# Rotary attention in a small transformer tower: which engine copies the transposed probabilities out of PSUM

## The chip, the cores and the metric

One core of a Trainium2 chip runs the whole program in one launch. The metric is the device time of one execution in microseconds; a kernel's time is the median of its runs.

## The reference

The input is 128 images. Each is cut into L = 82 overlapping patches and becomes 82 rows of D = 64 numbers. Four blocks follow, each added to its input and fed with a LayerNorm of it: an attention with relu in place of softmax, a mixture of 6 experts, an attention with rotary positions, and a mixture of 8 experts. The change touches the rotary attention alone. For one image, cut to what matters:

```python
q = concat([c_q @ Wqc, rope(c_q @ Wqr)])        # 48 plain and 16 rotated columns
k = concat([c_kv @ Wkc, rope(c_kv @ Wkr)])
v = c_kv @ Wv
wei = where(causal, q @ k.T / sqrt(64), -inf)   # 82 x 82
out = softmax(wei) @ v
```

All of it is in fp32.

## The kernel before, in words

The rows of all images stay in SBUF, in `h` (82 partitions, 128 images, 64 columns). Each stage walks through NG = 16 groups of G = 8 images. The program is written out by hand for every engine: each stage has one generator per engine (`scalar`, `tensor`, `vector`, `gpsimd`), which issues instructions in a fixed order and waits on semaphores. `build` steps these generators with `go`, so that the end of one stage is interleaved with the start of the next on each engine. An engine works strictly in its own order; a wait at its head holds up all that is behind it.

The rotary attention is `stage_rope_attention`. In iteration g the engines do the following, each in this order.

TensorE: `score(g)` (L1042, 16 matmuls of queries by keys into two PSUM banks), `turn_p(g-1)` (L1052, eight transposes of the exponentials of the group before, into `p_bank`, two other banks), `turn(g+3)` (L1010, transposes of normalised rows), `project(g+2)` (L1018 and L1020), `mix(g-1)` (L1065, eight images of probabilities by values, in 16 rows of the trace), `place(g+2)` (L1026, puts the rotated part into its columns) and `project_v(g+2)` (L1032). `mix(g-1)` waits for the copied probabilities (`p_ready`), for `copy_x(g+3)`, and for an earlier use of its bank. In iteration 14 `score(15)` stands behind `turn_p(13)`, and iteration 15 has no `score`.

VectorE: `mask(g)`, three dependent instructions (L1114 adds the causal bias to the scores and moves them to SBUF, L1116 takes the maximum of each row, L1118 scales it into `low`), then `rope_parts(g+2)` (L1108, reads the result of L1020; `place` waits for it), `statistics(g-2)` (L1133), `add(g-1)` (L1122 reciprocal of the sums, L1125 multiplies the mix by it, L1128 adds it to `h`) and, in four iterations, steps of a LayerNorm (`after_dve`: the variance in 1 and 9, `vary`, L525 to L531; the inverse root in 2 and 11, `invert`, L545 to L549). Iteration 14 masks both group 14 and group 15.

ScalarE: `copy_p(g-1)` (L969, the transposed probabilities from `p_bank` to `pt` in SBUF), `copy_x(g+3)` (L954), `raise_(g)` (L976, eight exponentials with their row sums, which wait for `low`), `copy_qk(g+2)` (L959), `copy_v(g+2)` (L964). Twice a square root for a LayerNorm comes between (L536), with a load of activation tables before and after it.

GpSimd: the normalisation of a group three ahead, two instructions each (L560 and L563, in the last stage L567), let go by the transposes L1010 or L1481.

What sets the order at the handover to the last stage (`stage_moe` with `layer` 1) is the list of `go` calls in `build`. VectorE runs iteration 14 of the attention, then `take_logits(0)` (L1689, reads the router's result L1493), iteration 15 with `add(14)`, `take_logits(1)` and the first step of the routing, `statistics(14)`, more of the routing, and `add(15)`. TensorE's transposes of the last stage (L1481) and its logits (L1493) share one bank, so each L1481 waits for the L1689 before it. ScalarE copies the transposed x of the last stage at L1375.

Of the kernel before, what the change touches and what calls it, by code (L numbers as in the profile page):

```python
# [18 lines left out]
ACT = mybir.ActivationFunctionType  # L19
# [6 lines left out]
L = (T - PW) // SW + 1  # L26
D = 64
G = 8
NG = B // G
# [65 lines left out]
def exists(g):  # L95
    return 0 <= g < NG


def wait(eng, sem, value):

    if value > 0:
        eng.wait_ge(sem, value)
# [27 lines left out]
def slots(t, g):  # L130

    return t[:, g * G:g * G + G, :]


def slot(t, g, b):
    return t[:, g * G + b, :]
# [755 lines left out]
def stage_rope_attention(nc, stack, new_sem, psum, h, stats, ident, W, mine, following, Z, before):  # L892
# [4 lines left out]
    def sem(name):  # L897
        return new_sem("sa_" + name)
# [16 lines left out]
    qk_bank, p_bank = psum[:, 2:4, 0:HALF], psum[0:L, 4:6, 0:HALF]  # L915
# [3 lines left out]
    v, pt = Z.v, Z.pt  # L919
# [13 lines left out]
    p_turned = sem("p_turned")  # L933
    p_ready = sem("p_ready")
    mixed = sem("mixed")
# [15 lines left out]
    def scalar(act):  # L951
        def copy_x(g):
            act.wait_ge(x_turned, g + 1)
            act.activation(xt[g % 2][:], xo_bank[:, 0:HALF], ACT.Copy).then_inc(x_ready, 1)  # L954

        def copy_qk(g):
            act.wait_ge(qk_done, g + 1)
            wait(act, scored, g - 1)
            act.activation(qk[g % 2][:], qk_bank, ACT.Copy).then_inc(qk_ready, 1)  # L959

        def copy_v(g):
            act.wait_ge(v_done, g + 1)
            wait(act, mixed, g - 3)
            act.activation(v[g % 4][0:L, :], rv_bank[0:L, :], ACT.Copy).then_inc(v_ready, 1)  # L964

        def copy_p(g):
            act.wait_ge(p_turned, g + 1)
            wait(act, mixed, g - 1)
            act.activation(pt[g % 2][0:L], p_bank.rearrange("p c (b l) -> p c b l", l=L), ACT.Copy).then_inc(p_ready, 1)  # L969

        def raise_(g):
            act.wait_ge(shifted, g + 1)
            wait(act, p_turned, g - 1)
            wait(act, shared, g - 1)
            for b in range(G):
                act.activation(prob[g % 2][:, b, :], masked[g % 2][:, b, :], ACT.Exp, bias=low[g % 2][:, b:b + 1], scale=SCALE,  # L976
                               accum_out=total[g % 2][:, b:b + 1]).then_inc(raised, 1)

        copy_x(0)
        copy_x(1)  # L980
        yield

        act.activation(unused[:], W.bias[:, 0:1], ACT.Exp)
        copy_qk(0)
        copy_v(0)
        copy_x(2)
        copy_qk(1)
        copy_v(1)

        for g in range(NG):  # L990
            if exists(g - 1):
                copy_p(g - 1)
            if exists(g + 3):
                copy_x(g + 3)
            yield
            raise_(g)
            if exists(g + 2):
                copy_qk(g + 2)
                copy_v(g + 2)
            LayerNorm.after_act(act, g, mine, following)  # L1000
            yield
        copy_p(NG - 1)

    def tensor(pe):
        def turn(g):
# [98 lines left out]
    def vector(dve):  # L1104
        def rope_parts(g):
            dve.wait_ge(r_done, g + 1)
            wait(dve, qk_done, g)
            dve.tensor_tensor(turned[:], rv_bank[:, 0:HALF].rearrange("p (j l) -> p j l", l=L),  # L1108
                              rope[:].unsqueeze(1).broadcast_to([128, NPAIR, L]), ALU.mult).then_inc(r_turned, 1)

        def mask(g):
            dve.wait_ge(scored, g + 1)
            wait(dve, raised, G * g - G)
            dve.tensor_tensor(masked[g % 2][:], s_bank, bias[:].unsqueeze(1).broadcast_to([L, G, L]), ALU.add).then_inc(biased, 1)  # L1114
            dve.wait_ge(biased, g + 1)
            dve.tensor_reduce(top[:], masked[g % 2][:], AX_X, ALU.max).then_inc(topped, 1)  # L1116
            dve.wait_ge(topped, g + 1)
            dve.tensor_scalar(low[g % 2][:], top[:], -SCALE, None, ALU.mult).then_inc(shifted, 1)  # L1118

        def add(g):  # L1120
            dve.wait_ge(raised, G * g + G)
            dve.reciprocal(share[:], total[g % 2][:]).then_inc(shared, 1)  # L1122
            dve.wait_ge(shared, g + 1)
            dve.wait_ge(mixed, g + 1)
            dve.tensor_tensor(mixed_sb[:], xo_bank[0:L, :].rearrange("p (b d) -> p b d", d=D),  # L1125
                              share[:].unsqueeze(2).broadcast_to([L, G, D]), ALU.mult).then_inc(scaled, 1)
            dve.wait_ge(scaled, g + 1)
            dve.tensor_tensor(slots(h, g), mixed_sb[:], slots(h, g), ALU.add).then_inc(added, 1)  # L1128

        def statistics(g):  # L1130
            dve.wait_ge(added, g + 1)
            for b in range(G):
                ins = dve.bn_stats(slot(stats, g, b), slot(h, g, b))  # L1133
            if g == NG // 2 - 1:
                ins.then_inc(following.counted, 1)

        rope_parts(0)
        yield
        rope_parts(1)

        for g in range(NG):
            if exists(g + 1):
                mask(g)
            if g == NG - 2:
                mask(NG - 1)
            if exists(g + 2):
                rope_parts(g + 2)
            if exists(g - 2):
                statistics(g - 2)
            if exists(g - 1):  # L1150
                add(g - 1)
            LayerNorm.after_dve(dve, g, mine, following)
            yield
        statistics(NG - 2)
        yield
        add(NG - 1)

    S = Tiles()
    S.gpsimd, S.scalar, S.tensor, S.vector = gpsimd, scalar, tensor, vector
    S.v_ready, S.biased, S.scaled = v_ready, biased, scaled  # L1160
    return S
# [706 lines left out]
```

## Time and profile before

| what | value |
|---|---|
| median of 3 runs | 713.41 us (712.61 to 719.24) |
| the profiled execution, its own time | 714.3 us |
| its span, first to last instruction | 712.4 us |
| mean granted TensorE clock | 0.939 |
| TensorE busy with matmuls | 604.7 us, 85% of the span |
| VectorE busy | 507.1 us, 71% |
| ScalarE busy | 318.6 us, 45% |
| GpSimd busy | 148.0 us, 21% |
| rotary attention, first mask to last mix | 423.9 to about 534.6 us |

PE is TensorE, PEld its weight loads, DVE is VectorE, ACT is ScalarE, POOL is GpSimd. A row of a timeline gives its start in us from the start of the span, its length in us, engine, line and operation, what it writes and reads, and in brackets how long the engine had been idle before it and what released it. L12 is line 12 of the kernel.

### The profile page before, as it was taken

What the parts mean: (1) busy time and instruction counts of PE and PEld (TensorE: products, weight loads), DVE (VectorE), ACT (ScalarE), POOL (GpSimd) and SP (SyncE); (2) the same over time, 40 slices, a digit from 0 to 9 for tenths busy, and PEclk for the clock granted to TensorE, in tenths of its full rate; (3) what the DMA queues carried; (4) which work ended last, traced back from release to release, by engine and by line L of the source; (5) the groups of instructions that cost most, each with busy time, mean ns of one, the idle gap of its engine ahead of it and who ended that gap; (6) DMA issues with size and microseconds to landing.
All of it is one profiled execution on the core that took longest, in us unless ns stands there. A gap on an engine that the chain in (4) does not pass through costs nothing.

```text
span 712.4 us, 17541 instructions
## 1 busy us (share of the span) xinstructions
PE 604.7 (85%) x6943; PEld 377.3 (53%) x6943; DVE 507.1 (71%) x1451; ACT 318.6 (45%) x738; POOL 148.0 (21%) x151
## 2 busy tenths in 40 slices
PE   1999999899986978888887889999967788889884
PEld 1985655479874433444433357877763434444441
DVE  3767789567846556777668457878867878888863
ACT  0100021043333574565666639888752534434441
POOL 1000004835362003121003042331332032210000
PEclk9999999999997797999999999999955989989998
DMA  9999863000000000000000000000000000000011
GB/s 298 412 385 285 271 235 115 2 1 2 1 3 0 2 1 1 2 1 1 3 1 1 1 1 2 2 2 2 1 1 2 11 12 20 20 14 19 21 24 26
DMA packets 28897, 39.19 MB, mean 55 GB/s; under 512 B 19984, under 2 KB 20368, under 8 KB 28816
## 3 DMA queue, kind: packets, MB, share of 16 engines
q1 hardware_dynamic: 19232, 35.46, 14.0%
q10 hardware_dynamic: 9584, 2.61, 1.9%
q8 instruction: 56, 0.92, 0.6%
q14 instruction: 25, 0.20, 0.1%
HBM read 35.37 MB, written 2.69 MB: 53 GB/s over the span
## 4 chain that ended last, share of the span: by engine, by line
PE 60%; DVE 21%; issue 8%; ACT 8%; DMA 2%; POOL 0%; SPq 0%; DVEq 0%; ACTq 0%; POOLq 0%
PE bank L404 12%; PE bank L1518 8%; PE bank L1556 4%; DVE m_hm L1767 3%; PE bank L1554 3%; PE bank L1579 3%; PE bank L816 3%; ACT m_h L1412 2%; PE bank L1065 2%; PE bank L1528 2%; PE bank L1539 2%; DVE cols L445 2%; PE bank L1486 2%; PE bank L1018 2%; PE bank L1507 2%
## 5 line engine op out<-in xcount | busy, mean ns | idle before, releaser
L560 POOL TENSOR_TENSOR centred<-h,mean 82x512 f32<-82x512 f32 x64 | 72.1, 1127 | 478.9 <-DVE rstd L549 281.2
L1405 ACT ACTIVATE m_h<-bank,m_b 128x656 f32<-128x656 f32 x112 | 90.4, 807 | 137.9 <-PE bank L1518 137.7
L1767 DVE TENSOR_TENSOR m_hm<-bank,m_h 128x656 f32<-128x656 f32 x112 | 93.7, 837 | 67.6 <-PE bank L1528 67.5
L404 PE MATMUL bank<-cols,tok_weight 64*64 64x328 f32 (+1 forms) x1800 | 116.0, 414 | 19.5 <-DVE cols L446 18.4
L404 PEld LDWEIGHTS bank<-cols,tok_weight 64*64 64x64 f32 x1800 | 76.9, 137 | 54.2 <-issue 16.7
L1518 PE MATMUL bank<-m_xt,m_w 64*64 64x328 f32 x896 | 95.1, 498 | 8.9 <-ACT m_h L1405 8.0
L445 DVE COPY cols<-image 128x1992 f32<-128x1992 f32 x32 | 62.1, 1950 | 17.1 <-DMA image<-in_x_dram 14.6
L1518 PEld LDWEIGHTS bank<-m_xt,m_w 64*64 64x64 f32 x896 | 25.2, 140 | 55.3 <-issue 28.8
L1554 PE MATMUL bank<-m_hm,m_wo 64*64 64x328 f32 x512 | 51.0, 469 | 2.7 <-DVE m_osb L1774 2.3
L1528 PE MATMUL bank<-ct,m_sel 64*64 64x328 bf16 x448 | 38.1, 322 | 14.3 <-DVE m_hm L1767 13.2
L976 ACT ACTIVATE sa_prob<-sa_masked,sa_low 82x82 f32<-82x82 f32 x128 | 44.6, 351 | 8.0 <-DVE sa_low L1118 8.0
L1412 ACT ACTIVATE m_h<-bank,m_b 128x328 f32<-128x328 f32 x96 | 45.7, 528 | 3.1 <-PE bank L1539 3.0
L1556 PE MATMUL bank<-m_hm,m_wo 128*64 128x328 f32 x192 | 39.4, 491 | 5.2 <-DVE m_hm L1767 5.2
L380 ACT ACTIVATE tok_fm<-bank,tok_bias 128x328 f32<-128x328 f32 x16 | 7.7, 531 | 78.0 <-issue 39.7
L1528 PEld LDWEIGHTS bank<-ct,m_sel 64*64 64x64 bf16 x448 | 15.0, 112 | 42.6 <-issue 27.4
L1539 PE MATMUL bank<-m_h,m_w 64*64 64x328 f32 x384 | 37.1, 458 | 0.0
L563 POOL TENSOR_TENSOR xn<-centred,rstd 82x512 f32<-82x512 f32 x32 | 35.0, 1093 | 2.5
L567 POOL TENSOR_TENSOR xn<-centred,rstd 82x512 f32<-82x512 f32 x32 | 34.0, 1061 | 2.5
L1507 PEld LDWEIGHTS bank<-ident,cp 82*96 82x96 bf16 x256 | 14.5, 128 | 34.8 <-issue 33.0
L1507 PE MATMUL bank<-ident,cp 82*96 82x82 bf16 x256 | 17.9, 219 | 16.7 <-DVE h L1781 14.4
L1579 PE MATMUL bank<-ident,m_osb 128*82 128x128 f32 x128 | 21.8, 297 | 9.8 <-DVE m_lg L1692 8.6
L451 DVE COPY h<-bank 82x512 f32<-82x512 f32 x16 | 10.3, 686 | 27.0 <-PE bank L398 27.0
(173 smaller groups left out, 1073.7 us busy)
## 6 DMA issues: line engine op xcount, KB each, us to landing
image<-in_x_dram SPq DMA_DIRECT2D x32, 1000.0 KB, 11.2
out_dram<-m_fin SPq DMA_DIRECT2D x16, 164.0 KB
tok_weight<-in_L_tok_weight_dram ACTq DMA_DIRECT2D x2, 400.0 KB, 8.3
m_w<-in_L_ffn_w_dram ACTq DMA_DIRECT2D x2, 128.0 KB
m_sel_raw<-c_sel_dram ACTq DMA_DIRECT2D x1, 256.0 KB
m_w<-in_L_ffn_expert_w_dram ACTq DMA_DIRECT2D x2, 96.0 KB
m_wo<-in_L_ffn_expert_w_dram ACTq DMA_DIRECT2D x4, 48.0 KB
m_sel_raw<-c_sel_dram ACTq DMA_DIRECT2D x1, 192.0 KB
```

The source lines that it names most:

```text
L404: return pe.matmul(sum_bank[u % 2][s][t * D:(t + 1) * D, L * j0:L * j1], weight[s * R:(s + 1) * R, c, :], cols[u % 2][s * R:(s + 1) * R, c ...
L445: dve.tensor_copy(dst[:, :, :, 0:NBLOCK - 1], src[:, :, 0:(NBLOCK - 1) * SW].rearrange("p k (m c) -> p c k m", c=SW))
L560: pool.tensor_tensor(self.centred[:], slots(self.h, g), mean.broadcast_to([L, G, D]), ALU.subtract).then_inc(self.shifted, 1)
L1405: act.activation(h1[n % RING][:], h1_bank, ACT.Gelu if last else ACT.Relu, bias=W.b1[:, k:k + 1]).then_inc(h1_ready, 1)
L1412: ins = act.activation(h2[n % RING][:, s, :], h2_bank[:, s, :], ACT.Relu, bias=W.b2[:, s, k:k + 1])
L1507: mm = pe.transpose(back[0:NR, b * L // 2:(b + 1) * L // 2].bitcast(BF16), cp[:, G * (g % 2) + b].rearrange("p i c -> p (i c)"), ident16[0 ...
L1518: mm = pe.matmul(h1_bank[e * D:(e + 1) * D, s, :], W.w1[rows, 2 * k + e, :], xt[g % len(xt)][rows, :], start=True, stop=True)
L1528: mm = pe.matmul(cb_bank[e * D:(e + 1) * D, s, :], W.sel[rows, 128 * k + D * e:128 * k + D * e + D], ct[g % 2][rows, s:G:2, :], start=True ...
L1539: mm = pe.matmul(h2_bank[at * D:(at + 1) * D, s, :], W.w2[rows, k, :], h1[n % RING][rows, s, :], start=True, stop=True)
L1554: mm = pe.matmul(o_banks[e][cols, :], W.wo[rows, 0, k, :], hm[k][rows, s, :], start=(k == 0), stop=False)
L1556: mm = pe.matmul(o_bank[cols, 0:HALF], W.wo[:, s, k, :], hm[k][:, s, :], start=(k == 0), stop=False)
L1767: dve.tensor_tensor(hm[k][:], cb_bank, src[n % RING][:], ALU.mult).then_inc(hm_ready, 1)
```

## The change

`copy_p` moves from ScalarE's generator to VectorE's. There it is a `tensor_copy` with the same waits and the same semaphore, and stands behind `mask(g)` (in iteration 14 behind both masks) and ahead of `rope_parts(g+2)`. The last one, `copy_p(15)`, stands ahead of `statistics(14)`.

```diff
@@ scalar
-        def copy_p(g):
-            act.wait_ge(p_turned, g + 1)
-            wait(act, mixed, g - 1)
-            act.activation(pt[g % 2][0:L], p_bank.rearrange("p c (b l) -> p c b l", l=L), ACT.Copy).then_inc(p_ready, 1)
...
         for g in range(NG):
-            if exists(g - 1):
-                copy_p(g - 1)
             if exists(g + 3):
                 copy_x(g + 3)
             yield
...
             yield
-        copy_p(NG - 1)
@@ vector
+        def copy_p(g):
+            dve.wait_ge(p_turned, g + 1)
+            wait(dve, mixed, g - 1)
+            dve.tensor_copy(pt[g % 2][0:L], p_bank.rearrange("p c (b l) -> p c b l", l=L)).then_inc(p_ready, 1)
...
             if g == NG - 2:
                 mask(NG - 1)
+            if exists(g - 1):
+                copy_p(g - 1)
             if exists(g + 2):
                 rope_parts(g + 2)
...
             LayerNorm.after_dve(dve, g, mine, following)
             yield
+        copy_p(NG - 1)
         statistics(NG - 2)
```

## Rows read from the trace of the kernel before

**Rows 1.** Windows: us, busy us of each engine (instructions), clock, DMA share, GB/s

```profile
443.60:482.00 38.40, 38.40 (x376) 30.53 (x374) 30.77 (x92) 30.87 (x122) 14.34 (x14) 1.00 0.01 2
520.00:553.00 33.00, 24.02 (x168) 17.40 (x172) 22.15 (x69) 11.50 (x31) 8.65 (x8) 0.50 0.01 2
```

**Rows 2.** Chain of waits from 443 to 458 us, shares by line

```profile
by line: PE bank L1018 22.9%; PE bank L1065 15.4%; PE bank L1032 13.8%; PE bank L1052 12.6%; PE bank L1020 11.0%; PE bank L1026 10.0%; PE bank L1042 10.0%; PE bank L1010 5.7%
```

**Rows 3.** Timeline of one middle group, 449 to 456 us

```profile
449.18 0.84 DVE L1114 TENSOR_TENSOR sa_masked<-bank,sa_bias 82x656 f32<-82x656 f32 x1 [0.64 <-PE bank L1042]
...
449.87 0.71 ACT L969 ACTIVATE pt<-bank 82x656 f32<-82x656 f32 x1 [0.32 <-PE bank L1052]
...
450.92 0.34 DVE L1118 TENSOR_SCALAR sa_low<-sa_top 82x8 f32<-82x8 f32 x1
...
451.64 1.32 PE L1065 MATMUL bank<-v,pt 128*82 128x64 f32 x16
...
452.89 0.82 PE L1026 MATMUL bank<-sa_turned,sa_place 64*128 64x328 f32 x4
...
455.54 0.84 DVE L1114 TENSOR_TENSOR sa_masked<-bank,sa_bias 82x656 f32<-82x656 f32 x1 [0.64 <-PE bank L1042]
```

**Rows 4.** Groups by line and form: busy us, mean ns of one, idle us before

```profile
L969 ACT ACTIVATE pt<-bank 82x656 f32<-82x656 f32 x16 | 11.3, 708 | 11.2 <-PE bank L1052 11.2
...
L451 DVE COPY h<-bank 82x512 f32<-82x512 f32 x16 | 10.3, 686 | 27.0 <-PE bank L398 27.0
...
L1689 DVE COPY m_lg<-bank 82x64 f32<-82x64 f32 x16 | 3.4, 212 | 0.4 <-PE bank L1493 0.4
```

**Rows 5.** Timeline of VectorE: first mask with a mix behind it, LayerNorm groups, g=14

```profile
429.76 0.84 DVE L1114 TENSOR_TENSOR sa_masked<-bank,sa_bias 82x656 f32<-82x656 f32 x1 [1.76 <-PE bank L1042]
...
486.04 0.69 DVE L1128 TENSOR_TENSOR h<-sa_mixed,h 82x512 f32<-82x512 f32 x1
...
488.39 0.84 DVE L1114 TENSOR_TENSOR sa_masked<-bank,sa_bias 82x656 f32<-82x656 f32 x1
...
490.13 0.17 DVE L1118 TENSOR_SCALAR sa_low<-sa_top 82x8 f32<-82x8 f32 x1
490.21 0.50 DVE L1108 TENSOR_TENSOR sa_turned<-bank,sa_rope 128x328 f32<-128x328 f32 x1
...
499.24 0.69 DVE L1128 TENSOR_TENSOR h<-sa_mixed,h 82x512 f32<-82x512 f32 x1
...
501.30 0.83 DVE L1114 TENSOR_TENSOR sa_masked<-bank,sa_bias 82x656 f32<-82x656 f32 x1
...
503.03 0.68 DVE L1118 TENSOR_SCALAR sa_low<-sa_top 82x8 f32<-82x8 f32 x1
...
513.67 0.84 DVE L1114 TENSOR_TENSOR sa_masked<-bank,sa_bias 82x656 f32<-82x656 f32 x1 [0.64 <-PE bank L1042]
```

**Rows 6.** Timeline of TensorE: a mix that was waited for, g=11

```profile
497.06 1.36 PE L1065 MATMUL bank<-v,pt 128*82 128x64 f32 x16 [0.70 <-ACT sa_xt L954]
498.34 0.82 PE L1026 MATMUL bank<-sa_turned,sa_place 64*128 64x328 f32 x4
```

**Rows 7.** Timelines of VectorE and TensorE, handover to the last stage

```profile
517.25 0.93 DVE L1118 TENSOR_SCALAR sa_low<-sa_top 82x8 f32<-82x8 f32 x1
...
519.32 0.69 DVE L1125 TENSOR_TENSOR sa_mixed<-bank,sa_share 82x512 f32<-82x512 f32 x1
...
520.65 0.21 DVE L1689 COPY m_lg<-bank 82x64 f32<-82x64 f32 x1
...
521.01 0.78 PE L1481 MATMUL bank<-ident,xn 82*128 82x82 f32 x4 [3.40 <-DVE m_lg L1689]
521.59 1.30 PE L1052 MATMUL bank<-ident,sa_prob 82*82 82x82 f32 x8
...
524.02 1.30 PE L1493 MATMUL bank<-m_wr,m_xt 128*82 128x16 f32 x8 [1.13 <-ACT m_xt L1375]
525.16 2.48 PE L1065 MATMUL bank<-v,pt 128*82 128x64 f32 x16
```

## The prediction

> **What bounds the kernel now.** I read the view of windows first, for the stretch of the rotary attention. TensorE is busy all of 38.40 us at full clock, VectorE and ScalarE 80% each [rows 1]. So the stage looks as if VectorE had room for one more copy a group (it idles 7.6 us in six groups, 1.3 us each). The chain of waits over two groups says the same from the other side: every step of it is a matmul line, and neither the copy of probabilities (L969) nor any line of VectorE is on it [rows 2]. The third view, the timeline of one group, tells what share of that idle time is of use, and the prediction rests on it. I measure all times in a group from M, the start of its mask (L1114). The masks start at 449.18 and 455.54, so a group takes 6.36 us [rows 3]. ScalarE starts the copy at M+0.69 and ends it at M+1.40, during the projections. TensorE's mix of the same probabilities (L1065) starts at M+2.46, right behind those projections, the placing of the rotated part (L1026) at M+3.71, the next mask 2.65 us behind that. The copy thus has about a microsecond to spare. VectorE at that time is in its mask: three instructions one behind the other until the lower bound (L1118) ends at M+2.08.
>
> **The change, part by part.**
> *Removed.* ScalarE loses 16 copies of 0.71 us, 11.3 us in all [rows 4]. In the middle groups this is worth nothing, since the mask's result, and not ScalarE's own work, releases the exponentials, and they are through well before their turn.
>
> *Added.* VectorE gets 16 copies of 82x656 from PSUM, a form that isn't in the trace. Its own copies from PSUM took 686 ns for 512 elements and 212 for 64 [rows 4]: 1.06 ns an element more, so 686 + 144 x 1.06 = 838 ns; the mask, which reads the same shape from PSUM, took 0.84 us [rows 3]. I take 0.84. The bounds: 0.71 (what ScalarE needs) and 0.93 (should the two-bank pattern cost a tenth more, an estimate over the 0.84). The Trainium skill (VectorE: DVE Perf Modes, the section on the TRN2 errata) puts a copy from PSUM at 120 + elements cycles of 0.96 GHz, here 776 cycles or 0.81 us, and says under "Why PSUM operands drop a tier" that the double rate of a copy in fp32 is lost with a PSUM operand. The rows agree with this within 4%; by the page's figure the sum below would be some 0.4 us smaller.
>
> *Moved.* The copy stands behind the three mask instructions in VectorE's order. It doesn't depend on them, and an instruction that doesn't depend on the one before starts 0.08 us before that one's end (L1118 at 490.13 for 0.17, L1108 at 490.21) [rows 5]. In the group of rows 3 it runs from M+2.00 to M+2.84. TensorE answers VectorE 0.15 us later (L1689 ends at 520.86, L1481 starts at 521.01) [rows 7]. So the mix starts at M+2.99, not at M+2.46, and after a stall it takes 1.28 us to the next line (497.06 to 498.34) [rows 6], not 1.25. The placing comes at M+4.27, 0.56 late, and with it everything up to the next mask: 6.92 us a group. Queued behind the copy on VectorE are the rotation of the next keys and queries, the statistics and the addition. The rotation starts at M+2.76 and ends 1 us before the placing wants it. The addition would wait for the late mix and ends near M+6.2, still ahead of the next mask. VectorE isn't the bound; the order of its queue is.
>
> *The thirteen periods.* Where TensorE carries the loop, a period is the end of L1118 after M plus 4.84 (-0.08 + 0.84 + 0.15 + 1.28 + 2.65). L1118 takes 0.34 in the groups like rows 3 (five, g=4 to 8), which ends at M+2.08 and gives 6.92. It takes 0.17 in g=10 and 13 (ends M+1.91): 6.75. It takes 0.67 in g=3 and 0.68 in g=12 (ends M+2.41): 7.25 [rows 5]. In four groups LayerNorm work hangs behind the addition and carries the loop: from the last addition (L1128) to the next mask 2.35 us with the variance (486.04 to 488.39; g=1, 9) and 2.06 with the reciprocal (499.24 to 501.30; g=2, 11) [rows 5]. Late mix start, 1.36 for it [rows 6], 0.11 to the multiplication, 0.73 for that: 7.45 and 7.54 (variance), 7.07 twice (reciprocal). Sum: 5 x 6.92 + 2 x 6.75 + 2 x 7.25 + 7.45 + 7.54 + 2 x 7.07 = 91.7. Before, the same 13 periods are 513.67 - 429.76 = 83.9 [rows 5]. Added: 7.8 us. Some groups pay more than 0.56, since TensorE had run ahead of a late mask there and now can't.
>
> *The last groups.* In g=14 the copy stands behind two masks: L1118 of the second ends at 518.18, M+4.51 [rows 7]. The copy ends at M+5.27, the mix at M+6.78, the multiplication starts at M+6.89, and the read of the first router logits (L1689) 1.33 later, as 519.32 to 520.65 [rows 7], at M+8.22. Before it was M+6.98: +1.2. From there ScalarE's relief pays. TensorE's second logits (L1493) waited 1.13 us for the copy of x, which stood behind the copy of probabilities on ScalarE [rows 7]. That goes; the probabilities of g=14 are turned by 522.89, VectorE is idle there and copies at once, and the mix starts at 523.93 where it was 525.16 [rows 7]: -1.2. The copy of g=15 falls behind a routing step of VectorE, an estimated +0.2 (bounds 0 and one copy, 0.84). All that follows hangs on that mix and shifts with it.
>
> *The clock.* TensorE's granted clock is 0.50 from 520 to 553, half of the 2.4 GHz [rows 1], after 3.4 us of idleness [rows 7]. Now a wait of about 3.2 us comes before the mix of g=13, so the fall to 1.2 GHz can come earlier, with that mix and the logits behind it at half clock: 2.48 against 1.36 for the mix [rows 6, 7], with the logits 0 to 1.7 us. I take half, 0.8. In the middle groups TensorE stands still 0.5 us in 6.9, and I expect no fall.
>
> Sum: 7.8 + 1.2 - 1.2 + 0.2 + 0.8 = 8.8 us. The profiled execution took 714.3 us with a span of 712.4, so it would take 723.1. It lay 0.9 above the median of the runs, 713.4, so the median I predict is 722.2. For the uncertain terms: an answer of TensorE 0.1 us slower or the copy at 0.93 adds about 1 us each; the copy at 0.71 takes 1.5 off, the clock's term 0.8 either way. The likeliest case's own range is 719.5 to 725.5.
>
> **Rivals.**
> *The copy costs half.* If VectorE moved two elements at once, the copy would take about 0.47 us (838 less half of 656 x 1.06, and a little for the odd end), and each of 13 periods and the last group lose 0.37 less. The middle groups then add 0.2. Sum 8.8 - 14 x 0.37 = 3.6, or 717.0. Against it: no copy or mask from PSUM in rows 4 goes faster than 1.06 ns an element.
> *GpSimd holds the copy up.* L1118 takes 0.17 when GpSimd is quiet and 0.34 to 0.93 when it runs [rows 5, 7]: it waits for the end of a GpSimd instruction. Should the copy wait too, for GpSimd's second instruction, which ends at about M+3.2, it would start 1.2 us late in some nine groups: +11 us, 733. Against it: the mask and the copies that read PSUM show no such spread.
> *The clock stays up* (the side of no loss). The change splits the one pause of TensorE at the handover to the mixture of experts into two, 3.2 and about 1.2 us. If neither let the clock fall, a mix there would take 1.36 and not 2.48 [rows 6, 7]. TensorE is busy 24.0 of the 33 us at half clock [rows 1]; at that ratio the same work takes 10.8 us less, and should four fifths of it be on the path (an estimate: in g=14 and 15 nearly every step waits for TensorE), 8.7 us come back. That cancels the loss: 713.5, not slower. It decides from the point where g=13's mix comes soon enough. Against it: the wait ahead of it is nearly as long as the pause after which the clock fell.
>
> **How the numbers follow.** The forecast has 0.72, the half-price copy 0.08, GpSimd 0.06, the clock 0.05; 0.09 stays for sizes in between, mostly on the low side, since stalls that two queues share can cost less than their sum. The range for 8 in 10 is 717 to 727. What a measurement of this kernel can tell from no change is about 1%, 7.1 us: slower by more means over 720.5. Of the forecast's own spread (its term for the clock, the answer time, the copy) some 0.85 lies above that, which is 0.61; GpSimd adds 0.06 and the sizes in between 0.03: 0.70. Within 1% are the rest of the forecast (0.11), the half-price copy (0.08), most of the clock's case (0.04) and of the sizes in between (0.04): 0.27. Faster by over 1%: 0.03, what is left of these two.
>
> **What would show it.** In the profile after, masks 6.9 us apart in the middle of the stage; L1065 idle before it near 0.5 us each time, released by VectorE's copy; the copy at 0.84; ScalarE waiting longer for the mask; L1128 ending ahead of the next mask; TensorE's wait for L1375 gone. If the masks stay 6.4 apart, the order of the queue didn't matter and the reading of rows 3 is wrong. If the copy varies from group to group, GpSimd is in it. If the masks stand apart as forecast and the total doesn't, look at the clock and the logits from 518 us on.

## The result and the profile after

The changed kernel took 726.9 us, the median of 4 runs (724.8 to 729.4). The kernel before took 714.6 (four runs: the three of above and one more, 715.7). The ratio is 1.0164 with an interval of 1.0098 to 1.023, which is 7 to 16 us more. The forecast was 8.8 us more and 722.2 us, the range 717 to 727. In a second series the changed kernel took 726.5 in 6 runs against 718.4 in 23, ratio 1.0158 (1.0106 to 1.0209). A ratio here compares the means of the runs that lie within 1.5% of their kernel's fastest, which leaves out 9 of the 23 and none of the 6; the means of all runs of that series are 726.8 and 718.4, a difference of 8.4 us and a ratio of 1.0116.

The profiled execution took 729.4 us with a span of 727.6, so 15.2 more than the 712.4 of before. That is nearly twice the forecast, and the first thing to do is to cut the span into three at points both traces have: the first mask, and the start of the last mix.

(The stage in the table of the kernel before ends with the end of that mix, here it ends with its start.)

| part of the span, us | before | after | difference | forecast |
|---|---|---|---|---|
| ahead of the first mask | 423.9 | 430.5 | +6.5 | 0 |
| rotary stage, first mask to the start of the last mix (g=15) | 108.2 | 116.3 | +8.0 | +8.8 |
| behind the last mix | 180.2 | 180.9 | +0.6 | 0 |

The code of the first part is the same in both kernels. The experiments below show that its time differs by more than 6.5 us between executions of kernels that are alike in it.

In the middle of the stage the change is seen where the forecast had it. The timeline of the changed kernel for one middle group (line numbers have moved: L1106 is the mask that was L1114, L1110 the lower bound, L1125 VectorE's copy, L1057 the mix, L1018 the placing):

```profile
457.86 0.84 DVE L1106 TENSOR_TENSOR sa_masked<-bank,sa_bias 82x656 f32<-82x656 f32 x1 [1.06 <-PE bank L1034]
...
459.60 0.34 DVE L1110 TENSOR_SCALAR sa_low<-sa_top 82x8 f32<-82x8 f32 x1
459.77 0.71 PE L1012 MATMUL bank<-sa_xt,sa_w 128*128 128x328 f32 x2
459.85 0.83 DVE L1125 COPY pt<-bank 82x656 f32<-82x656 f32 x1
...
460.61 0.48 DVE L1100 TENSOR_TENSOR sa_turned<-bank,sa_rope 128x328 f32<-128x328 f32 x1
...
460.78 1.36 PE L1057 MATMUL bank<-v,pt 128*82 128x64 f32 x16 [0.30 <-issue]
...
462.07 0.82 PE L1018 MATMUL bank<-sa_turned,sa_place 64*128 64x328 f32 x4
```

Set it against [rows 3], with M = 457.86. The copy was at M+0.69 on ScalarE, now it is at M+1.99 on VectorE, right behind L1110. The mix was at M+2.46 and is at M+2.92, 0.10 us after the copy's end. The placing was at M+3.71 and is at M+4.21. The next mask comes at 464.72: 6.86 us a group, 6.36 before. The bracket behind the mix says "issue", not L1125. The profile names no releaser for that wait, and a reader who goes by the names alone would not find VectorE guilty. From the start of the projection L1012 to the mix it is 1.01 us, and 0.55 before (L1020 at 451.09): the mix is held up 0.46 us, more than the bracket's 0.30, and the placing follows it 0.04 later than it did, which makes the 0.50 of the period. The times name the releaser: the mix starts 0.09 to 0.10 us after the copy's end in every middle group.

The chain of waits of the changed kernel between 457 and 472 us shows the same hole, twice, as a step of its own ahead of L1057. VectorE's lines are not on it, as they were not in [rows 2]:

```profile
459.93 0.55 PE bank L1012 x2
460.49 0.30 issue
460.78 1.36 PE bank L1057 x16
462.14 0.75 PE bank L1018 x4
```

By line and form of the changed kernel (columns as in [rows 4]): the copy costs 829 ns. TensorE's mixes are preceded by 9.0 us of idle time. VectorE waits 13.7 us for the scores, 9.4 before: with one instruction more a group it idles longer ahead of its mask, since TensorE comes later.

```profile
L1057 PE MATMUL bank<-v,pt 128*82 128x64 f32 x256 | 24.9, 258 | 9.2 <-issue 9.0
...
L1106 DVE TENSOR_TENSOR sa_masked<-bank,sa_bias 82x656 f32<-82x656 f32 x16 | 13.4, 836 | 13.8 <-PE bank L1034 13.7
L1125 DVE COPY pt<-bank 82x656 f32<-82x656 f32 x16 | 13.3, 829 | 2.1 <-PE bank L1044 2.1
```

Windows of the changed kernel (columns as in [rows 1]), six groups of the middle and the handover. TensorE is busy 96% of the first where it was 100%, still at 2.4 GHz; in the second its clock is half, as before:

```profile
457.86:499.61 41.75, 39.98 (x382) 30.41 (x382) 35.38 (x104) 27.83 (x114) 12.49 (x12) 1.00 0.01 2
532.00:567.00 35.00, 26.77 (x188) 20.36 (x192) 25.85 (x81) 10.88 (x35) 8.65 (x8) 0.51 0.01 1
```

The handover in the changed kernel, VectorE and TensorE, from the mask of g=14 (527.27) on, against [rows 7]:

```profile
530.85 0.92 DVE L1110 TENSOR_SCALAR sa_low<-sa_top 82x8 f32<-82x8 f32 x1
...
531.69 0.83 DVE L1125 COPY pt<-bank 82x656 f32<-82x656 f32 x1
...
532.62 2.29 PE L1057 MATMUL bank<-v,pt 128*82 128x64 f32 x16 [3.11 <-issue]
...
536.34 0.21 DVE L1689 COPY m_lg<-bank 82x64 f32<-82x64 f32 x1
...
536.70 0.78 PE L1481 MATMUL bank<-ident,xn 82*128 82x82 f32 x4 [0.76 <-DVE m_lg L1689]
537.27 1.30 PE L1044 MATMUL bank<-ident,sa_prob 82*82 82x82 f32 x8
...
538.37 1.22 PE L1493 MATMUL bank<-m_wr,m_xt 128*82 128x16 f32 x8
538.61 0.84 DVE L1125 COPY pt<-bank 82x656 f32<-82x656 f32 x1 [2.06 <-PE bank L1044]
...
539.55 2.47 PE L1057 MATMUL bank<-v,pt 128*82 128x64 f32 x16
```

TensorE waits 3.11 us for the copy behind the two masks and then runs the mix mostly at half clock, in 2.29 us. Its second logits (L1493) follow the turned probabilities with no wait; before they waited 1.13 for ScalarE.

### The profile page after: what moved, and what is told of

Same layout as the page of the kernel before. It is cut to its first block, busy times and chain, and to the rows that moved or that the text cites. A ratio compares the mean times of both kernels' runs of the same rounds, so it can differ in the third digit from the quotient of the medians.

```text
span 727.6 us, 17541 instructions
## 1 busy us (share of the span) xinstructions
PE 615.9 (85%) x6943; PEld 381.2 (52%) x6943; DVE 518.5 (71%) x1467; ACT 310.9 (43%) x722; POOL 147.5 (20%) x151
## 3 DMA queue, kind: packets, MB, share of 16 engines
q1 hardware_dynamic: 19232, 35.46, 13.7%
## 4 chain that ended last, share of the span: by engine, by line
PE 64%; DVE 20%; issue 8%; ACT 5%; DMA 2%; POOL 0%; DVEq 0%; SPq 0%; ACTq 0%; POOLq 0%
PE bank L404 12%; PE bank L1518 8%; PE bank L1556 4%; PE bank L1057 3%; DVE m_hm L1767 3%; PE bank L1554 3%; PE bank L1579 3%; PE bank L816 3%; PE bank L1010 2%; PE bank L1024 2%; ACT m_h L1412 2%; PE bank L1528 2%; PE bank L1486 2%; PE bank L1539 2%; DVE cols L445 2%
## 5 line engine op out<-in xcount | busy, mean ns | idle before, releaser
L560 POOL TENSOR_TENSOR centred<-h,mean 82x512 f32<-82x512 f32 x64 | 70.0, 1094 | 497.2 <-DVE rstd L549 287.9
L404 PE MATMUL bank<-cols,tok_weight 64*64 64x328 f32 (+1 forms) x1800 | 118.6, 421 | 20.1 <-DVE cols L446 19.5
L404 PEld LDWEIGHTS bank<-cols,tok_weight 64*64 64x64 f32 x1800 | 77.8, 139 | 56.5 <-issue 19.4
L445 DVE COPY cols<-image 128x1992 f32<-128x1992 f32 x32 | 62.1, 1953 | 17.2 <-DMA image<-in_x_dram 15.2
L563 POOL TENSOR_TENSOR xn<-centred,rstd 82x512 f32<-82x512 f32 x32 | 36.6, 1143 | 2.5
L567 POOL TENSOR_TENSOR xn<-centred,rstd 82x512 f32<-82x512 f32 x32 | 33.9, 1061 | 2.5
L1057 PE MATMUL bank<-v,pt 128*82 128x64 f32 x256 | 24.9, 258 | 9.2 <-issue 9.0
L1057 PEld LDWEIGHTS bank<-v,pt 128*82 128x82 f32 x256 | 23.0, 172 | 15.8 <-issue 15.7
```

The source lines that it names most:

```text
L404: return pe.matmul(sum_bank[u % 2][s][t * D:(t + 1) * D, L * j0:L * j1], weight[s * R:(s + 1) * R, c, :], cols[u % 2][s * R:(s + 1) * R, c ...
L445: dve.tensor_copy(dst[:, :, :, 0:NBLOCK - 1], src[:, :, 0:(NBLOCK - 1) * SW].rearrange("p k (m c) -> p c k m", c=SW))
L560: pool.tensor_tensor(self.centred[:], slots(self.h, g), mean.broadcast_to([L, G, D]), ALU.subtract).then_inc(self.shifted, 1)
L1057: mm = pe.matmul(xo_bank[0:L, D * b:D * b + D], pt[g % 2][:, b, :], v[g % 4][:, image(b)], start=True, stop=True)
```

## The experiments

The theory is that of the prediction: the copy's place in VectorE's queue makes the mix late. Its rivals are VectorE's load as such, the clock at the handover, and for the excess over the forecast a slower first part.

**Both kernels once more.** No edit.

> The changed kernel once more. Its profiled execution took 15.2 us more than that of the kernel before, of which 8.0 lie between the first mask and the last mix of the rotary stage, 6.5 ahead of the first mask in code that the change doesn't touch, and 0.6 behind. Theory A (the 6.5 us are the spread of executions): the stage from first mask to last mix takes 116.3 us again (108.2 before), the first mask comes anywhere from 423 to 431 us, and the ratio of the times is about 1.012 (8 to 9 us). Theory B (the changed program is slower ahead of the stage too): the first mask again comes near 430 and the ratio is near 1.02.

> The kernel before once more, to see the spread. Theory A: the ratio's interval holds 1.000, the stage from first mask to last mix takes 108.2 us within 0.2, and the first mask moves by some us between executions. Theory B: the first mask comes at 424 us within 1 us every time.

The stage took 115.5 us in the changed kernel and 108.2 in the kernel before. The first mask came at 433.1 and at 429.5, where it had been 430.5 and 423.9. The kernel before against itself has a ratio of 0.9981 (0.9932 to 1.0031), the changed one 1.0158. The first mask of the kernel before moved by 5.5 us between two executions, which refutes theory B's fixed 424 us. Theory B for the changed kernel had its first mask near 430 again, and it came at 433.1. Against that theory stand three kernels below that are the changed one but for the handover or a second copy behind the mask: their first masks came at 420.7, 425.9 and 428.8. Over all thirteen profiled executions of this study with a usable trace it came between 420.5 and 433.1, and the part behind the last mix took 177.6 to 189.9 us, though the kernels are alike in both parts. The stage in between repeats to 0.02 us where the code is the same and the clock falls at the same place. So I judge by the stage, and by ratios only where they are clear. Theory A expected a ratio near 1.012; 1.0158 is above that, its interval includes it, and the means of all runs have 1.0116.

The thirteen periods of the changed kernel took 90.98 us in both executions. The stage's 0.8 us between 116.3 and 115.5 is the clock: in the second execution it fell later. There the mix of 13 took 1.50 us and the two rows below are 6.15 us apart (the first execution: 6.93). The timeline of that second execution:

```profile
535.28 1.50 PE L1057 MATMUL bank<-v,pt 128*82 128x64 f32 x16 [3.11 <-issue]
...
541.43 2.47 PE L1057 MATMUL bank<-v,pt 128*82 128x64 f32 x16
```

**The copy ahead of the maximum.** The same copy on the same engine, in another place of the queue.

```diff
             dve.tensor_tensor(masked[g % 2][:], s_bank, ...).then_inc(biased, 1)
+            if between is not None:
+                copy_p(between)
             dve.wait_ge(biased, g + 1)
             dve.tensor_reduce(top[:], ...).then_inc(topped, 1)
```

> VectorE's copy stands between the first and the second instruction of the mask (behind L1114, ahead of the maximum), and not behind the third. Theory 1 (the place in VectorE's queue costs the time): the copy ends near M+1.65, the mix no longer waits for it, a middle group takes 6.36 us again, the LayerNorm groups lose up to 0.6 each since VectorE carries them, and the handover gains 1.2: the stage takes 108 to 110 us, and the kernel is within 0.3% of the kernel before. Rival (VectorE's added work costs the time, or its copy is slow for TensorE wherever it stands): a middle group stays at 6.8 to 6.9 us and the stage at 115 to 117.

The stage took 108.63 us, the thirteen periods 84.75 (83.91 before), and the ratio is 0.9976 (0.9932 to 1.002). The timeline of this kernel, a middle group with M = 446.43:

```profile
446.43 0.84 DVE L1106 TENSOR_TENSOR sa_masked<-bank,sa_bias 82x656 f32<-82x656 f32 x1 [0.54 <-PE bank L1034]
...
447.19 0.83 DVE L1127 COPY pt<-bank 82x656 f32<-82x656 f32 x1
...
447.94 0.82 DVE L1110 TENSOR_REDUCE sa_top<-sa_masked 82x8 f32<-82x656 f32 x1
...
448.79 0.84 DVE L1112 TENSOR_SCALAR sa_low<-sa_top 82x8 f32<-82x8 f32 x1
448.90 1.32 PE L1057 MATMUL bank<-v,pt 128*82 128x64 f32 x16
...
452.80 0.84 DVE L1106 TENSOR_TENSOR sa_masked<-bank,sa_bias 82x656 f32<-82x656 f32 x1 [0.20 <-PE bank L1034]
```

The copy ends at M+1.59, the mix starts at M+2.47 without a wait, and the group takes 6.37 us. VectorE does all the work of the changed kernel; the loss in the middle is gone. This is the run that settles the cause: it is the place, not the load. VectorE now waits only 0.20 us for the scores, so it is near its own limit: of the groups with LayerNorm work two grew (g=2 6.88 from 6.50, g=9 7.83 from 7.39), one shrank (g=11 7.28 from 7.58). The handover took 0.4 us less than before, where 1.2 was expected. L1112 takes 0.84 here, 0.34 before; in its new place it meets GpSimd's second instruction, and the copy beside GpSimd's first takes its usual 0.83.

**The middle alone, the handover alone.** VectorE copies the groups for which the condition holds, ScalarE the others, each at its old place.

```diff
+    def by_vector(g):
+        return g <= 12          # g == 13 and g == 14 in the two that follow
```

> VectorE copies the groups 0 to 12, ScalarE the groups 13 to 15 as before. Theory: the thirteen periods from the first mix's mask to that of group 14 take 91.0 us as in the changed kernel (83.9 before), and the handover from there to the last mix takes 18.5 us as before: +7.1 us in all. Rival (the handover, with its copy behind two masks and the earlier fall of the clock, carries a good part of the loss): clearly under +6.

> VectorE copies group 13 alone, ScalarE the other fifteen. Theory: the thirteen periods stay at 83.9 us; the copy stands behind both masks of iteration 14, so the mix of group 13 starts 5.3 us behind the mask of group 14, not 2.07, with the clock falling ahead of it as in the changed kernel; ScalarE's copy of group 14 keeps TensorE's second logits waiting as before, so from the mix of 13 to that of 14 it takes about 8 us (9.4 before, 6.2 to 6.9 in the changed kernel), and the stage is 109.7 to 110.5 us (108.2 before). Rival (the pause TensorE has there anyway swallows the late mix): 108.2.

> VectorE copies group 14 alone. Theory (ScalarE's copy of group 14 stood ahead of its copy of x, for which TensorE's second logits waited 1.1 us): the mix of group 14 comes about 1.2 us sooner, 8.2 us behind that of group 13 and not 9.4, the rest of the stage is as before: 107.0 us, and the kernel is 1.2 us faster. Rival (something else holds TensorE there): 108.2 us.

| us | before | changed | 0 to 12 | 13 | 14 |
|---|---|---|---|---|---|
| thirteen periods (g=1 to 13) | 83.9 | 91.0 | 91.0 | 83.9 | 83.9 |
| mask of 14 to mix of 13 | 2.07 | 5.35 | 2.07 | 5.35 | 2.07 |
| mix of 13 to mix of 14 | 9.42 | 6.93 | 9.41 | 8.40 | 8.11 |
| mix of 14 to mix of 15 | 7.00 | 7.17 | 7.01 | 7.00 | 6.99 |
| stage | 108.2 | 116.3 | 115.3 | 110.5 | 106.9 |

The parts add: +7.1, +2.3 and -1.3 make 8.1, with the last copy's 0.17 8.2, and the whole change has +8.0. The rivals fall: the handover does not swallow the late mix of 13 (+2.3), and with +1.0 for 13 and 14 together it does not carry most of the loss. The ratio of the kernel with groups 0 to 12 is 1.0141 (1.0065 to 1.0217). The kernel with group 13 alone ran once, in 731.0 us, of which 189.9 lie behind the last mix (180.2 before); that total says nothing of the change. In the kernel with group 14 alone the second logits follow the turned probabilities at once. In this timeline L1506 is the logits line:

```profile
525.21 0.78 PE L1494 MATMUL bank<-ident,xn 82*128 82x82 f32 x4 [3.40 <-DVE m_lg L1702]
525.78 1.30 PE L1056 MATMUL bank<-ident,sa_prob 82*82 82x82 f32 x8
526.88 1.21 PE L1506 MATMUL bank<-m_wr,m_xt 128*82 128x16 f32 x8
528.06 2.47 PE L1069 MATMUL bank<-v,pt 128*82 128x64 f32 x16
```

Its total doesn't show the gain: 719.9 us in 4 runs against 715.9, ratio 1.0103 (1.0017 to 1.0189). The stage of its profiled execution is 1.3 us shorter, its first mask came at 428.2. An effect of this size can't be read from four totals, and such an interval of a ratio can miss: I expected less than 1 by 0.2%.

**The copy twice.** The second waits for the first, and only the second lets TensorE go.

```diff
-            dve.tensor_copy(pt[g % 2][0:L], ...).then_inc(p_ready, 1)
+            dve.tensor_copy(pt[g % 2][0:L], ...).then_inc(p_once, 1)
+            dve.wait_ge(p_once, g + 1)
+            dve.tensor_copy(pt[g % 2][0:L], ...).then_inc(p_ready, 1)
```

> The changed kernel with every copy made twice on VectorE, the second waiting for the first; only the second releases TensorE. Theory (every us that VectorE takes ahead of the mix comes out whole in the period): 0.83 and some 0.05 of waiting more a group, so a middle group takes 7.7 us (6.86 in the changed kernel), g=10 and 13 about 7.55, the LayerNorm groups about 0.8 more each, the thirteen periods near 102 us. Rival (part of the copy is hidden still): clearly less than 0.8 a group.

A middle group takes 7.73 us, 0.87 more than in the changed kernel, and the second copy starts 0.86 after the first. All of it comes out in the period, and nothing is hidden. The thirteen periods took 103.8 us (the kernel's one run 736.3). Of the 1.8 above what I expected, 1.6 are in one group, g=3, which took 9.62 where 7.18 and 0.87 would be its share: the clock fell to 1.2 GHz in it. Windows of this kernel around it:

```profile
440.00:447.00 7.00, 5.20 (x50) 3.73 (x47) 6.73 (x14) 3.78 (x15) 3.85 (x4) 1.00 0.01 2
447.00:451.00 4.00, 4.00 (x25) 3.00 (x24) 2.52 (x12) 1.65 (x7) 0.31 (x1) 0.57 0.00 2
```

TensorE had been busy 5.2 of the 7 us ahead of the fall; it stayed at 2.4 GHz in the other groups of this kernel and in all middle groups of the changed one.

**Matmuls into the pauses.** To price the clock, TensorE multiplies something that nobody reads while it would wait. The first kernel has nine calls ahead of the mix of 13; the two short fillings have five there, one behind the first logits and three behind the mix of 14; the last two kernels, where ScalarE copies group 13 and the mix is early, have none there, five behind the first logits and the same three.

```diff
+        def fill(n):
+            for i in range(n):
+                pe.matmul(qk_bank[:, i % 2, :], w[:, 0, :], xt[(NG - 1) % 2][:], start=True, stop=True)
...
+            if g == NG - 2:
+                fill(9)                  # 5 in the two short fillings, 0 in the last two kernels
             if exists(g - 1):
                 mix(g - 1)
+            if g == NG - 1:              # in all four later kernels
+                fill(3)
...
+            if last and f == 1:          # last stage, behind the first logits; in all four later kernels
+                for i in range(1):       # 5 in the last two kernels
+                    pe.matmul(h1_bank[0:2 * EP, i % 2, :], W.wr[:], xt[0][:], start=True, stop=True)
```

> The changed kernel with nine matmuls more on TensorE (128x328 each, 0.29 us, into banks that nothing reads any more) in the 3.1 us in which it waits for the copy of group 13. Theory (the early fall of the clock costs the handover): the mix of 13 runs at full clock, 1.3 us and not 2.3, the logits behind it 0.7 and not 1.25, and from that mix to the one of group 14 it takes about 1.5 us less than the 6.93 of the changed kernel; the clock falls later or stays up, and then the mixes of 14 and 15 take 1.3 us too and the last part of the stage gets shorter by up to 2 us. Rival (the clock falls for a reason of its own, or costs nothing here): the mix of 13 at 2.3 us and no change.

The filling was too long: a call in fp32 is two rows of the trace, eighteen for nine calls, and they took 5.17 us where I had reckoned 2.6. The mix of 13 came at 7.07 behind the mask and not 5.35. It ran at full clock, in 1.32 us, and from it to the mix of 14 it took 5.14 us. The stage took 114.9 us with 1.7 us of my own delay in it, in a run of 724.8 us, the only one.

> The changed kernel with matmuls more in TensorE's pauses at the handover, sized to end ahead of what it waits for (a call in fp32 is two rows of 0.29 us): five calls ahead of the mix of 13, one behind its logits, three behind the mix of 14. The nine calls of the run before were 5.2 us long and delayed the mix by 1.7. Theory (the clock costs up to 1.7 us at the mix of 13 and more behind it): the mix of 13 starts 5.35 us behind the mask and at full clock, 13 to 14 takes 5.2 us, 14 to 15 takes 5.2 to 5.9, and the stage 113 to 114 us (116.3 and 115.5 in the two executions of the changed kernel). Rival (the pauses hide the half clock): 115.5.

> The run before once more, since its profiled execution took 1145.8 us, all of it slower, and its trace tells nothing. Theory: as before, the mix of 13 starts 5.35 us behind the mask at full clock, 13 to 14 takes about 5.2 us, the stage 113 to 114 us, and the ratio is about 1.005 to 1.008 (1.016 for the changed kernel). Rival: 115.5 us and 1.01.

The first gave a ratio of 1.0053 (1.0007 to 1.0099); its profiled execution took 1145.8 us and is not read. TensorE was slow in it at a granted clock of 1.00 (the median matmul of L404 took 779 ns, in all other traces 435), VectorE was not (512 us busy, 507 in the kernel before); why is open. The second has a trace. TensorE at the handover:

```profile
524.79 2.96 PE L1062 MATMUL bank<-sa_xt,sa_w 128*128 128x328 f32 x10
528.06 1.36 PE L1057 MATMUL bank<-v,pt 128*82 128x64 f32 x16 [0.31 <-issue]
529.25 0.71 PE L1501 MATMUL bank<-m_wr,m_xt 128*82 128x16 f32 x8
...
533.23 1.36 PE L1057 MATMUL bank<-v,pt 128*82 128x64 f32 x16 [0.25 <-issue]
...
539.10 2.34 PE L1057 MATMUL bank<-v,pt 128*82 128x64 f32 x16 [0.95 <-issue]
```

The mix of 13 is at the same 5.34 behind the mask, now in 1.36 us; 13 to 14 takes 5.17 us (6.93 and 6.15 unfilled), 14 to 15 5.87 (7.17). The stage is 113.2 us. The half clock thus costs the changed kernel at least 2.3 to 3.1 us inside the stage (the last mix ran at it here too), of which the early fall is 0.8. The rest is no loss by the change: the kernel before runs its last two mixes at half clock as well. The ratio is 1.0037 (0.9974 to 1.0099). The filling takes 2.3 to 3.1 of the stage's 7.2 to 8.0 us back, by another way than they came.

**The filling without the change, and the best of both.**

> The kernel before with such matmuls: five calls in the 3.4 us ahead of the second transposes, three behind the mix of 14. Theory: from the mix of 13 to that of 14 it takes about 7.3 us instead of 9.4 (each matmul at full clock, ScalarE's copies ahead of x as before), 14 to 15 about 5.2 to 5.9 instead of 7.0, the stage 105 us (108.2). Rival: 108.2.

> The same matmuls, and VectorE copies group 14 alone. Theory: the two gains add: 13 to 14 about 6.5 us, 14 to 15 5.2 to 5.9, the stage 104 us (108.2 before), and the kernel is faster than the kernel before by 4 us or more (0.6%), which the spread ahead of the stage may hide.

In the kernel before with the filling, 13 to 14 took 8.24 us, 14 to 15 7.89 and the stage 108.0. Its ratio is 0.9956 (0.9909 to 1.0003) over 10 runs, with a stage that gained 0.2 us. The stage is a miss: the clock fell after all, at the second mix, and the three calls behind it then took 3.6 us at half clock, longer than the pause of 1.8. With group 14's copy on VectorE as well, TensorE's 1.1 us wait for ScalarE went, the clock held longer, and the stage took 105.6 us: 7.27 and 6.44 for the two steps, 2.7 us better than before, not the expected 4. Its ratio is 0.9936 (0.9897 to 0.9975) over 12 runs, median 712.6 against 717.8. Its stage is the shortest of all, and its interval lies below 1. How much of the 0.6% is the stage's 2.7 us (0.4%) and how much chance, the totals don't tell: the kernel above it has 0.9956 for 0.2 us. Beside the changed kernel it was not run.

## Why the prediction was right

The direction was right, and the time was inside the range, though only by 0.1 us: 726.9 where the range ends at 727. That it did not fall outside is luck: the parts outside the stage decided it. The difference between the medians of the first series is 12.3 us where 8.8 was forecast, of the second 8.1. Inside the stage, where the mechanism is, the forecast was 8.8, and 8.0 came in the first execution, 7.2 in the second. Step by step:

- *What bounds the stage.* Right. The copy alone moved behind the mask makes the loss, and put ahead of the maximum it costs nothing in the middle groups. VectorE's idle 1.3 us in each group were real, in two pieces: 0.64 ahead of the mask [rows 3] and 0.58 behind it, from M+2.08 to M+2.67, as this row of the kernel before shows. Of the second piece 0.38 us lay ahead of the mix at M+2.46, less than half of a copy.

```profile
451.85 0.50 DVE L1108 TENSOR_TENSOR sa_turned<-bank,sa_rope 128x328 f32<-128x328 f32 x1 [0.58 <-PE bank L1020]
```

- *The copy's price.* 829 ns measured, 838 worked out from [rows 4]. The 0.81 us by the Trainium skill (VectorE: DVE Perf Modes, the section on the TRN2 errata) is 2 to 3% below what the trace shows, the 838 ns from the rows 1% above. All copies took 825 to 836 ns, so neither the half-price rival nor GpSimd's hold on the copy was there. The 0.34 of L1118 showed how GpSimd's hold looks; the copy from PSUM did not have it, though it ran beside GpSimd. In the kernel with the copy made twice, the second copy of a middle group starts at 462.81, inside a GpSimd instruction (462.09 to 463.13), and takes 0.84. The working of the half-price rival has a slip: 838 less half of 656 x 1.06 is 490 ns and not 470. Another is in the bounds, where a copy of 0.71 takes 14 x 0.13, 1.8 us, off and not 1.5. Neither moves the forecast.
- *The period.* 6.86 against 6.92. The start at M+1.99 was right to 0.01. TensorE's answer took 0.10 us, not 0.15, which is nearly all of the 0.7 us by which the thirteen periods (90.98, forecast 91.7) came out shorter. Singly: g=1 and 9 7.40 and 7.46 (7.45, 7.54), g=2 and 11 6.99 and 7.10 (7.07), g=3 and 12 7.18 (7.25), g=10 and 13 6.69 (6.75).
- *The last groups.* The mix of 13 at 5.35 (5.42). Where the clock fell late, the first logits were read at M+8.27, forecast 8.22 (538.22 less 529.95). The gain from ScalarE's relief: 1.3 us shown by the kernel with group 14 alone, forecast 1.2. The last copy: +0.17, forecast 0.2.
- *The clock.* Forecast 0 to 1.7, put in the sum as 0.8. The first execution had 0.8 and the second 0, with 8.0 and 7.2 us added in the stage. Without the clock's term the forecast is 8.0; of the 0.8 that the second lies below it 0.7 are in the thirteen periods, from TensorE's quicker answer.
- *The rival with no loss* asked that the clock stay up. It fell in all profiled executions of the changed kernel, as reckoned. With filled pauses it held until the last mix and saved 2.3 to 3.1 us in the stage. The rival's 8.7 were for 33 us, more than half of them behind the last mix, and there the clock was low in the filled kernel too (0.51 from 541 to 560 us); so its four fifths stay untested.

What failed is the step from the sum to the time: that the profiled execution stands to the median of the runs by a fixed 0.9 us. The first part alone, the same code in all these kernels, moves by 12 us between executions, and the median of three runs, 713.4, lay low: 23 runs later gave 718.4 for the same kernel. I had taken 1% as what can be told and kept the range at 10 us for reasons that were all inside the stage. The first ratio is worth 11.7 us, the second 11.3, all runs of the second series 8.4; the stage explains 7.2 to 8.0 of that. The spread covers the rest, but that the changed program isn't slower elsewhere by a us or two was not shown. Its ten runs took 724.5 to 729.4 us, a narrower spread than the kernel before's 708.6 to 726.8, and none was as fast as that kernel's fastest with the stage's loss added.

## What to carry to other kernels

An engine's idle share says nothing about where in its cycle the idle time lies. Before work is moved to it, write down, for one period, when the input is ready, when the queue ahead of the new instruction is through, and when the output is wanted; here that was M+0.65, M+2.0 and M+2.4 for a copy of 0.83. If the window is missed, look for an earlier slot in the same queue: between two dependent instructions of the mask the same copy was free in the middle groups.

And cut the span at points that the change can't move before a difference is explained. Here 6.5 of 15.2 us lay ahead of the first changed instruction.

## What the runs showed that I had not expected

- The spread of the parts that don't change: the first mask at 420.5 to 433.1 us, while the stage behind it repeated to 0.02 us. Part of it is TensorE's clock at the end of the first stage, whose last matmul (L404) started at 143.4 us in the kernel before, at 145.5 in its repetition and at 146.6 in the changed kernel. That is 2.1 of the 5.5 us between the first two and 3.2 of the 6.5 between the kernels; the rest came later. From 233 to 420 us the clock was 0.95 in the first of them and 0.91 in the two others. Windows of the kernel before, and then of its repetition (the clock is the third number from the right):

```profile
120.00:140.00 20.00, 17.13 (x226) 9.41 (x220) 15.34 (x44) 1.55 (x4) 17.58 (x17) 1.00 0.00 1
```

```profile
120.00:140.00 20.00, 16.31 (x196) 8.88 (x192) 15.15 (x43) 1.40 (x3) 15.90 (x16) 0.91 0.00 1
```

- With two copies a group the clock fell once in the middle of the stage, and cost 1.6 us there. More waiting of TensorE can cost more than its own length; how near the changed kernel is to that was not tried.
- A wait for another engine's copy can stand as "issue" in the profile's brackets and in the chain. In the changed kernel 9.0 us before the mixes do.
